# A transformer layer pair on one core: the table of where each routed row goes is made by one-hot products at the end of the first layer, and that layer's side work is set at other points of the attention heads

## What is computed

```python
# layer 0
x = x + 0.5 * ffn0(layernorm(x))      # dense 256x256 plus 8 rank-8 experts, top 2 of 8 gated by softmax
x = x + attn0(layernorm(x))           # 16 heads of 16, q/k/v/o with a rank-16 addition each
x = x + 0.5 * ffn0(layernorm(x))
# layer 1: each token goes to 4 given experts of 32 (topk_idx, topk_weight)
x = x + 0.5 * moe(layernorm(x))
x = x + latent_attn(layernorm(x))     # causal, 16 heads of 128+64, low-rank q and kv
x = x + 0.5 * moe(layernorm(x))
```

## Time and profile before

| what | us |
|---|---|
| median of 3 runs | 1529.6 |
| lowest and highest | 1526.13 and 1538.55 |
| the profiled execution, its own time | 1540.34 |
| span of its trace | 1538.4 |
| mean granted TensorE clock | 0.908 of full |
| busy: PE, DVE, ACT, POOL | 1260.5, 935.9, 676.8, 548.2 |

### The profile page before, as it was taken

The page is one execution under the profiler, slowest core; times in us unless marked ns, Lnnn a source line. Parts: engine busy times, 40 slices in busy tenths (PEclk is TensorE's granted clock), DMA queues, the critical chain, the costliest instruction groups (busy, mean ns, idle before and its releaser), DMA issues.

```text
span 1538.4 us, 21771 instructions
## 1 busy us (share of the span) xinstructions
PE 1260.5 (82%) x6361; PEld 798.1 (52%) x6362; DVE 935.9 (61%) x2702; ACT 676.8 (44%) x1706; POOL 548.2 (36%) x558
## 2 busy tenths in 40 slices
PE   6777888887777557999877899889889999599990
PEld 4432333333232446888744556546555656488870
DVE  7777576756754402232469887987888695232227
ACT  2124555454546114555324554455455353155550
POOL 2062251444443044555121211143134133455550
PEclk9887899998979879999999999999999999699995
DMA  4757074380221255454301000020001101355448
GB/s 119 117 90 204 27 93 169 55 212 21 89 78 50 116 201 178 154 162 149 128 28 42 15 28 0 2 88 21 1 18 39 55 22 55 137 162 163 149 135 276
DMA packets 80382, 147.99 MB, mean 96 GB/s; under 512 B 13885, under 2 KB 62078, under 8 KB 77326
## 3 DMA queue, kind: packets, MB, share of 16 engines
q1 hardware_dynamic: 62286, 104.41, 24.9%
q0 software_dynamic: 17408, 42.00, 7.7%
q10 hardware_dynamic: 576, 0.18, 0.0%
HBM read 83.21 MB, written 63.00 MB: 95 GB/s over the span
## 4 chain that ended last, share of the span: by engine, by line
PE 52%; DVE 31%; issue 7%; ACT 5%; DMA 2%; POOL 1%; SPq 1%; another core or an unknown queue 1%; DVEq 0%; POOLq 0%; ACTq 0%
PE m_psG L1073 11%; PE m_psY L1089 5%; DVE a_t L1508 4%; DVE a_mx L770 4%; PE a_psA L1267 3%; DVE a_nb L1516 3%; PE a_psO L425 3%; PE m_psX L1064 3%; PE a_psU L400 3%; PE a_psU L1249 3%; PE a_psS L411 2%; ACT a_pr L1378 2%; PE a_psU L1255 2%; PE a_psO L1290 2%; DVE a_q L1504 2%
## 5 line engine op out<-in xcount | busy, mean ns | idle before, releaser
L144 POOL DMA_INDIRECT outs_dram<-m_ys,dest x192 | 184.1, 959 | 166.2 <-ACT m_ys L1010 155.7
L1030 DVE TENSOR_TENSOR m_hm<-m_psG,m_sg 128x128 f32<-128x128 f32 x192 | 56.0, 292 | 283.4 <-ACT m_sg L1004 172.9
L1378 ACT ACTIVATE a_pr<-a_psA,a_nb 128x512 f32<-128x512 f32 (+3 forms) x256 | 132.6, 525 | 217.6 <-DVE a_nb L1516 216.7
L770 DVE TENSOR_REDUCE a_mx<-a_psU 128x1 f32<-128x512 f32 x256 | 165.4, 685 | 101.4 <-PE a_psU L400 83.1
L1434 POOL TENSOR_TENSOR a_q<-a_q,a_t 64x512 f32<-64x512 f32 x64 | 80.8, 1263 | 353.9 <-DVEq L1511 333.4
L1073 PE MATMUL m_psG<-arena,m_xgT 128*128 x768 | 205.0, 390 | 0.5 <-issue 0.2
L545 ACT ACTIVATE a_P<-a_psS 128x512 f32<-128x512 f32 x256 | 143.8, 597 | 92.9 <-PE a_psS L411 74.8
L144 POOL DMA_INDIRECT rows_dram<-a_xd,slot x128 | 125.1, 977 | 143.2 <-DVE a_xd L124 77.0
L400 PE MATMUL a_psU<-arena 96*128 96x512 bf16 x256 | 108.1, 429 | 47.0 <-DVE a_mx L770 37.8
L1073 PEld LDWEIGHTS m_psG<-arena,m_xgT 128*128 128x128 f32 x768 | 132.9, 193 | 16.2 <-issue 3.9
L1516 DVE TENSOR_REDUCE a_nb<-a_psA 128x1 f32<-128x512 f32 (+3 forms) x256 | 113.4, 485 | 36.3 <-PE a_psA L1269 26.8
(11 more groups left out here) (255 smaller groups left out, 2338.6 us busy)
## 6 DMA issues: line engine op xcount, KB each, us to landing
m_xg<-rows_dram SPq DMA_DIRECT2D x48, 512.0 KB
arena<-in_mo_w SPq DMA_DIRECT2D x9, 2048.0 KB
arena<-part_dram SPq DMA_DIRECT2D x96, 128.0 KB
rows_dram<-arena SPq DMA_DIRECT2D x12, 1024.0 KB
arena<-outs_dram SPq DMA_DIRECT2D x16, 512.0 KB, 3.5
part_dram<-a_part SPq DMA_DIRECT2D x16, 384.0 KB
m_xg<-outs_dram SPq DMA_DIRECT2D x8, 512.0 KB, 4.6
m_ys<-outs_dram SPq DMA_DIRECT2D x8, 512.0 KB, 5.1
```

What stands on the lines that cost most here:

```text
L144: pool.indirect_dma_start(out=rows_dram, out_offset=bass.IndirectOffsetOnAxis(ap=slot[:, c:c + 1], axis=0), in_=row, in_offset=None).then_ ...
L770: dve.tensor_reduce(mx[g % 2][:, 4 * kt + qt:4 * kt + qt + 1], psU[n % 2][:, :], AX, ALU.max).then_inc(u_free, 1)
L1378: ins = act.activation(pr[S % 2][:, AT[t]:AT[t] + (t + 1) * P], psA[:, AT[t]:AT[t] + (t + 1) * P], ACT.Exp, bias=nb[S % 2][:, t:t + 1], sc ...
```

## The change

Three things are changed in the first layer, and one in the layout of `outs_dram`.

**Where side work stands.** `F1` goes from 7 to 20 and `F2` from 25 to 33, so the second feed-forward of batch b begins at (b+2, 1) and not at (b+1, 25). The q/k/v work goes from points 0 to 8 to points 7 to 18. The four gate rows stand at four points and not at three, the gates are made in two parts at successive points, and the scales of a layer norm in two parts (`scales_begin`: aggregates, conversions and one Newton step; `scales_end`: two Newton steps) some points apart. The two output additions stand at one point.

**How `dest` is made.** `places`, `entry`, `table_dram`, `a_number` and L911 are gone. The slot number is split into its low 7 bits (row within a block) and the rest (block). For each quarter of the 64 columns DVE writes a one-hot of the low part (128x2048) and of the block (128x1536), the latter times the column number and times 64 times the partition, all bf16; PE adds the products of these over all 64 columns into psO, 32 matmuls of 128x96 per quarter; so psO[row, block] is the number of the output row for each used slot, and 0 for an empty one. `invert` puts a spare row there where it is 0. `outs_dram` is laid out for that: copy c of token p is at row 1 + 64p + c.

**Zeroing.** Six of the 12 DMAs that zero `rows_dram` come from a tile that POOL clears first of all (`blank`, in the P buffer) and stand ahead of the first pass; ACT's first exponential waits for them. The other six follow in pass 0. POOL's program is simpler: bias, then `route` in one piece, then `terms`, then the 16 row scatters in one piece.

```diff
     TO, NRM, SPLIT, MX = (1, 9, 17, 25), (2, 10, 18, 26), 0, (4, 12, 20, 28)
-    F1, F2 = 7, 25
-    QSC, QLN, QT, QK, QV = 0, 1, 2, 3, 7
-    AT, OP, OA, OST, OSC = 19, 20, 21, 23, 24
+    F1, F2 = 20, 33
+    TX, GM, GAP, GA, GB, TH, LM, LA, ST, SB, SE, XD = 1, (2, 3, 4, 5), 6, 7, 8, 9, 10, 11, {1: 12, 2: 13}, 14, 16, 18
+    QSC, QLN, QT, QK, QV = (7, 11), 13, 14, 15, 17
+    AT, OP, OA, OST, OSC = 19, 20, 21, 23, (29, 30)
...
+            pe.wait_ge(o_copied, GROUPS)
+            for q in range(QUARTERS):
+                pe.wait_ge(hots_ready, q + 1)
+                for c in range(HC):
+                    for n, right in enumerate((row_hot(q), col_hot(q))):
+                        ins = pe.matmul(psO[:, 0:NBLK], low_hot(q)[:, c * P:(c + 1) * P], right[:, c * NBLK:(c + 1) * NBLK],
+                                        start=(q == 0 and c == 0 and n == 0), stop=(q == QUARTERS - 1 and c == HC - 1 and n == 1))
+                ins.then_inc(inverted, 1)
...
+                        if st == 0 and c == 0:
+                            act.wait_ge(wiped[0], 16 * 6)
...
+            def low_ones(q):
+                dve.wait_ge(halves_ready, 1)
+                dve.wait_ge(pv_done, 4 * GROUPS)
+                if q >= 3:
+                    dve.wait_ge(inverted, q - 2)
+                c = slice(q * HC, (q + 1) * HC)
+                dve.tensor_tensor(low_hot(q).rearrange("p (c n) -> p c n", n=P), iota[:, 0:P].unsqueeze(1).to_broadcast([P, HC, P]),
+                                  low[:, c].unsqueeze(2).to_broadcast([P, HC, P]), ALU.is_equal)
+
+            def high_ones(q):
+                c = slice(q * HC, (q + 1) * HC)
+                link(dve.tensor_tensor(row_hot(q).rearrange("p (c n) -> p c n", n=NBLK),
+                                       iota[:, 0:NBLK].unsqueeze(1).to_broadcast([P, HC, NBLK]),
+                                       high[:, c].unsqueeze(2).to_broadcast([P, HC, NBLK]), ALU.is_equal))
+                link(dve.tensor_tensor(col_hot(q).rearrange("p (c n) -> p c n", n=NBLK), row_hot(q).rearrange("p (c n) -> p c n", n=NBLK),
+                                       iota[:, 1 + q * HC:1 + (q + 1) * HC].unsqueeze(2).to_broadcast([P, HC, NBLK]), ALU.mult))
+                dve.tensor_scalar(row_hot(q), row_hot(q), iota[:, P + 1:P + 2], None, ALU.mult).then_inc(hots_ready, 1)
+
+            def invert():
+                dve.wait_ge(spare_in, 16)
+                dve.wait_ge(inverted, QUARTERS)
+                link(dve.scalar_tensor_tensor(out=empty, in0=psO[:, 0:NBLK], scalar=0.0, in1=spares, op0=ALU.is_equal, op1=ALU.mult))
+                dve.tensor_tensor(dest[:, :], psO[:, 0:NBLK], empty, ALU.add).then_inc(dest_in, 1)
...
-                if i == 1 and p == 0:
-                    places()
+                if i == B and p == 0:
+                    halves()
+                if i == B and p == OP:
+                    low_ones(0)
+                    high_ones(0)
+                if i == B + 1 and p == F2 - PTS + 1:
+                    low_ones(1)
...
+            high_ones(1)
+            for q in range(2, QUARTERS):
+                low_ones(q)
+                high_ones(q)
+            invert()
...
-            for i in range(-2, B + 2):
+            for i in range(0, B + 2):
                 b = i + 1
-                if 1 <= b < B:
+                if i == 0:
+                    pool.wait_ge(rest_in, 16 * NREST)
+                if i < B:
+                    bias(i)
+                if i == 0:
+                    for part_of in range(3):
+                        route(part_of)
+                if b < B:
                     for c in range(4):
                         terms(b, c)
...
+                if 0 <= i - 2 < B:
+                    rows(i - 2, 0, TPB * TOPK)
...
-    return out_dram[t * P * TOPK:(t + 1) * P * TOPK, :].rearrange("(p k) d -> p (k d)", k=TOPK)
+    return out_dram[1:1 + P * NC, :].rearrange("(p c) d -> p (c d)", c=NC)[:, t * TOPK * D:(t + 1) * TOPK * D]
...
             for h in range(2):
                 sp.wait_ge(placed[h], 16 * TPB * TOPK * B // 2)
+            sp.wait_ge(dest_in, 1)
```

212 lines of the change are left out of this document (111 added, 101 removed).

## The result

The changed kernel takes 1523.2 us (median of 20 runs, 1520.7 to 1529.7), the kernel before 1531.0, timed beside it (20 runs, 1521.7 to 1538.6): ratio 0.9956, 95% interval 0.9939 to 0.9973. That is a gain of 7 us, clear of the noise but under 1%. Forecast were 1496 us and a gain of 34. The profiled executions differ by 16.5 us (1540.3 and 1523.8), more than the medians: that of before was 9 us above its median, that of after at it.

What follows compares the result with a forecast made beforehand. It took PE and DVE waiting for each other over lumpy work in the 144 points as the bound. -4 - 8.4 - 24 + 2 = -34 from 1540.3 gave 1506, scaled to the median 1496 us; range 1477 to 1524.

Steps and rivals of the forecast that it cites:

- rival A: In the points: the lumps of work only move to PE; gain 10 us at least, 1519 us, or 1523 with the tail; chance 0.17.
- 83 to 59 above the floor, a gain of 24: In the 144 points: time above the summed minimum of engine work per pair falls from 83 to 59 us, bounds 0 and 43.
- (a) to (c): Points' time above the floor: half clock 36 us, 22 left; POOL against DVE, 5 left; hand-overs and other stalls 38, 32 left.
- Ahead of the points, -4: Before the first point: `bases` and batch 1's statistics move behind the first two maxima, so this stretch is 4 us shorter.
- Zeroing 6 MB early ... 0: Before the points: early zeroing stands in SP's queue behind all first loads, beside DVE's and PE's work; 0, with 5 us allowed.
- Floor, -8.4: In the points: the sum over pairs of the largest of DVE, PE and ACT work or 3.3 us falls from 344.1 to 335.7.
- (a): In the points: PE's half clock adds 36 us above the floor, of which 22 were taken to stay.
- The entries, 0: POOL's 64 entries, 61.6 us, and their table load lay in gaps, so dropping them gains 0.
- End of the stage, +2: After the last normalisation: one-hots and inversion end about when the last scatter did; 2 us longer, bounds 0 and +10.
- rival B: End of stage: DVE's one-hot instructions hold POOL's scatters, 16 to 20 us on top, gain halved to 1513 us; chance 0.09.
- PE's loads under 60 us: Sign that the forecast is right: PE's loads wait under 60 us for DVE, where they stood 85.4 us before.
- DVE's longest run between maxima under 4 us: Sign that the forecast is right, in the points: DVE's longest run of work between two maxima stays under 4 us.

Runs made afterwards that it cites:

- experiment 1: The kernel before traced twice more with no edit: profiled executions of 1536.5 and 1532.1 us, beside 1540.3 in its first trace.
- g_no_entries: The kernel before without POOL's 64 entries into table_dram, so its output is another one: ratio 0.9997 to the kernel before.
- after_again: The changed kernel with no edit, traced and timed again on another chip as a control: ratio 0.9934 to the kernel before, points 381.9 us.
- k: The changed kernel with the row scatters of batches 0 and 1 spaced, two every two points: ratio 0.9775 to the kernel before.
- before_third: The kernel before with no edit, its third trace: profiled execution 1532.1 us, points 418.1 us.
- experiment 8: Two edits of the changed kernel, ratios to the kernel before: the zeros' memset on VectorE, 0.9941; three idle matmuls behind each of PE's first 28 maxima, 0.9960.
- l: The kernel before with a POOL wait ahead of each entry and each scatter of batches 0 and 1, meant to spread them: ratio 0.9988 to the kernel before.

## Why the prediction was wrong

The direction was right and the size was not: 7 us came for 34. 1523.2 lies at the very end of the range of 1477 to 1524, and inside it partly by luck: the high end was made for rival A and a longer tail, and only the tail came as said.

**The step that failed: 83 to 59 above the floor, a gain of 24.** I read all of the 83 us as half clock, POOL against DVE and hand-overs of this table, and counted the waits for `remote` to what "no order removes". Two other things were in them. Some 9 us were the excess of one execution (experiment 1), which the changed kernel's execution hadn't. And the waits for `remote` are holes beside and behind runs of indirect DMAs; the change made the runs longer, `rows(i - 2, 0, 16)` without a wait between the pieces, and so two long holes with half clock behind them. The changed kernel stood 67.4 us above the floor. With the old pieces it is 51.2, spaced 44.4: the long holes cost 16 to 23 us, and without them (a) to (c) end below the 59. But they also start below the 83: on the chip without holes it is 54.5 (g_no_entries, which has no entries) and 46.2 (after_again), 8 us for 24. So removing the burst makes up the forecast (k, 0.9775) on a chip where the kernel before keeps its slow stretches; it doesn't show that the table alone is worth what I said. Why the kernel before is 20 us slower in the points on the other chips is not shown; short holes and 104 to 120 us of half clock for 88 are what the traces have.

**The sum on the profiled executions.** 1506 were forecast and 1523.8 came, 18 more: 8 in the points (403.1 for 335.7 + 59), 4 ahead of them, 6 at the end of the stage. The other 10 to the median are the scaling by 0.993, which gave the changed kernel's execution an excess that it didn't have. With the 418 us of before_third, the points gain 15 us; less 8 at the end of the stage, that is the measured 7.

**Ahead of the points, -4.** Measured: 0. `bases` did move (the first point of pass 0 has it), but the new memset of `blank` stood ahead of V's, and DVE waited beside it. The step "Zeroing 6 MB early ... 0" looked at SP's queue and not at POOL's.

**Floor, -8.4.** No run measures it by itself. It isn't a strict bound either: for (1,24) with (1,25) it gives 7.6 us where the trace has 7.3. Of (a), the half clock of the first 14 points is free or nearly so (experiment 8).

**The entries, 0.** Right on the chip without holes (g_no_entries), not shown on the others.

**End of the stage, +2.** Measured +8.3: 5.8 us of stretched scatters, a third of what rival B put on it (16 to 20), and 2.5 us before `xd`, of which the +2 had 0 to 1.4.
**What I said would show it.** Points 390 to 402: 403.1. Clock above 0.9 in passes 1 to 3: 0.98, 0.89, 0.93. PE's loads under 60 us: 87.4, so false; but these waits didn't fall in the traces where the time did either, and are a poor sign. DVE's longest run between maxima under 4 us: 2.7 from pass 1 on, but 5.4 and 4.0 in pass 0, where `bases` now lies. Scatters 1.26 us apart: only the last eight, so B's sign came. First load behind the last scatter within 3 us: 2.4.

## What to carry over

A wait that looks useless (for a piece of scatters to land) may be what keeps a queue from running without a gap; when a change removes one, ask what shares anything with that engine, and look at long points where no engine waits for a named one. Before a gain is taken from the trace, trace the kernel before a second time: the excess of one execution lies somewhere, here in the very term that I wanted to shrink. Ask of a run that shall show a mechanism absent whether its edit did what it was made for: l did not spread most of its DMAs, and g ran on the one chip without holes. A time that no engine is named for is not a time that no change can touch. An engine's program has a head: a memset in front of it delays everything behind, and what stands beside it.
